# Graph attention passes: the segment's open-node factor is spread over partitions at the end of a round instead of the start of the next

## The chip, the cores and the metric

The kernel runs on one core of a Trainium2 chip, as one launch. The metric is the device time of that launch in microseconds (us). "Time before" is the median of three runs. The engines are named as the profile names them: PE is TensorE's matmul stream, PEld its weight loads, DVE is VectorE, ACT is ScalarE, POOL is GpSimd and SP the sync engine's DMA queue.

## The reference

The program computes four graph layers on 3125 nodes of 256 features and 50000 edges sorted by target node (`dst`), each followed by a residual and a layer norm. Two of the four are attention layers, and only these have to do with the change. Layer 1 has 4 heads of 64, layer 2 has 8 heads of 64. Cut to the core both do this:

```python
score = f(edge)                                    # [E, heads]
m     = segment_max(score, tgt, num_segments=n)
ex    = exp(score - m[tgt])
denom = segment_sum(ex, tgt)
alpha = ex / denom[tgt]
out   = segment_sum(alpha[..., None] * msg_edge, tgt)   # [n, heads, 64]
```

In layer 1 the score is a dot product of a gathered key row with the target's query, in layer 2 a leaky sum of one number of the source and one of the target.

## The kernel before, in words

Edges stand in NCH = 416 chunks of 128, grouped so that a chunk belongs to one tile of 128 target nodes. `Attend` runs one attention layer over all chunks; `Attend1` (4 heads) and `Attend2` (8 heads) set its tables. They are called the first and the second pass here. Work goes in NW = 26 rounds of WIN = 16 chunks. POOL gathers one row per edge into a ring of 36 slots. While round w is weighed and summed, the scores of round w + 1 are made.

A segment is a run of edges with one target node. The maximum of a segment may reach over several chunks and over a round's end. In every round a chain of small DVE steps (`CHAIN`, `chain`: "run", "most", "ends_in", "open", "ahead", "both", "picked", "edge", "most_1", "most_2", "fall", "below") finds the maximum of each segment inside the 16 chunks and the maximum carried in. Four PE instructions serve it (`TURNS`: "score", "ends", "spread", "back"). "fall" is by how much the maximum of the node that is still open at the round's start has risen since the round before. Its sum so far must be multiplied by exp(-fall), and all other nodes of that tile by 1.

Before the change that factor is made so:

- DVE compares `iota` with the open node's number (`seg.opens`, one column a round) right behind "ends_in": `open_hot`, heads x 128, at line 2238.
- ACT makes `other` = 1 - open_hot on one partition (line 2311, position `OTHER_AT`, 10 or 8 of 16). At position 14 it makes exp(-fall) and the diagonal matrix `diag` of it (lines 2314, 2316), and then the exponentials of the round's scores (line 2319).
- PE, at position 0 of the following round and behind the sum of chunk 15, multiplies open_hot by diag and adds other x ones (`scale_up`, lines 2369 and 2370). That gives a factor for each node and head in PSUM (bank `SMALL`, columns 128 on).
- DVE, at position 2, multiplies the accumulated tile by it (`rescale`, lines 2517 to 2521 and 2613 to 2619), before it adds chunk 0 of the round (`add_up`, lines 2515 and 2611).

The order on each engine is written out by hand: each engine has one program, in which the 16 positions i of a round are unrolled. PE at position i does the sum of the chunk before (`total(n - 1)`, lines 2512 and 2605), at i = 1, 5, 9, 13 four transposes for the one-hot rows of a later group (line 2334), then the fetches of query or score rows for the next round (lines 2457 and 2559), then a step of the chain, then at i = 0 `scale_up`. DVE at position i adds the chunk of two positions earlier. A sum may start when the add three chunks (first pass) or two chunks (second pass) before it is done (`SUMS`). An add waits for the add before it to have ended. ACT weighs the gathered rows of each chunk by its exponentials: in the first pass all four heads (line 2508), in the second four of the eight (line 2600), the other four being DVE's (line 2589). Every four chunks it casts the turned one-hots (line 2298).

The numbers of the open nodes come from `Segments`, once, while layer 1's tables are made: the local target number of each chunk's first edge is written to memory and read back onto 8 partitions (line 2037), and `vector_ends` copies each 16th to `opens` (line 2021).

Of the kernel before, what the change touches and what calls it, by code (L numbers as in the profile page):

```python
# [1944 lines left out]
class Segments:  # L1945
# [3 lines left out]
    def __init__(self, b, ctx, slot_rows):  # L1949
        sb = lambda n, s, d=F32: b.sb(n, s, d, ctx)  # L1950
        self.links = sb("links", [H2, NCH + 1, 2], BF16)
        self.opens = sb("opens", [H2, NW])
        self.masks = b.dram("masks", [NCH, 4 * P], BF16)
        self.hots = slot_rows.hots
        self.ends = b.dram("chunk_ends", [3, NCH])
        shared = [s for half in b.arrived for s in half]
        self.arrived = shared + [b.sem(f"slot{k}") for k in range(len(shared), RING)]
        self.before = [b.past] * len(shared) + [0] * (RING - len(shared))
        self.uses = [2 * len(range(k, NCH, RING)) for k in range(len(shared))]
        b.past = [b.past + n for n in self.uses]  # L1960
        self.passes, self.sems = 0, {}
        self.b = b
        self.turned, self.kept, self.stored, self.back = (b.sem(f"segments_{n}") for n in ("turned", "kept", "stored", "back"))
# [15 lines left out]
    def open_tables(self, b, own, spare, lent):  # L1979

        self.same = spare[0:CP, 0:3 * CG * P].rearrange("c (m g q) -> c m g q", m=3, g=CG)
        at = CG * P
        self.key = lent[0:CP, 0:at].rearrange("c (g q) -> c g q", g=CG)
        self.segs = lent[0:CP, at:3 * at].bitcast(BF16).rearrange("c (g m q) -> c g m q", g=CG, m=4)
        self.first, self.last, self.local_f = (lent[0:H2, 3 * at + k * NCH:3 * at + (k + 1) * NCH] for k in range(3))
        self.local_0 = b.sb("seg_local0", [CP, CG], F32, own)
# [26 lines left out]
    def vector_ends(self, e):  # L2013

        kept, finish = self.kept, self.finish
        e.wait_ge(self.back, 16 * 3)
        e.memset(self.links[:, 0, 0:1], 0.0)
        e.memset(self.links[:, NCH, 0:2], 0.0)
        e.tensor_tensor(self.links[:, 1:NCH, 0], self.first[:, 1:NCH], self.last[:, 0:NCH - 1], ALU.is_equal)
        e.tensor_tensor(self.links[:, 0:NCH, 1], self.first[:, :], self.last[:, :], ALU.is_equal)  # L2020
        e.tensor_copy(self.opens[:, :], self.local_f[:, 0:NCH:WIN]).then_inc(kept, 1)
        e.wait_ge(kept, 4)
        finish(e, self.links[:, :, :], self.links[:, :, :]).then_inc(kept, 1)
        e.wait_ge(kept, 5)

    def sync(self, e):
# [9 lines left out]
        e.dma_start(self.last[:, :], on_all(self.ends[1], H2)).then_inc(self.back, 16)  # L2036
        e.dma_start(self.local_f[:, :], on_all(self.ends[2], H2)).then_inc(self.back, 16)
        e.wait_ge(self.back, 48)


class Attend:


    def __init__(self, b, seg, own, name, heads, acc, table, word, stride, parts, x, lent=0):
# [23 lines left out]
        self.fall, self.keep_r, self.diag = sb("fall", [H, 1]), sb("keep_r", [H, 1]), sb("diag", [H, H])  # L2068
        self.open_hot, self.other = sb("open_hot", [H, P]), sb("other", [H, P])
        self.hot_in, self.mask_in = [sem(f"hot_in{k}") for k in range(self.HOTS)], [sem("mask_in0"), sem("mask_in1")]  # L2070
# [5 lines left out]
        self.hot_made, self.weighed, self.weighed_v = sem("hot_made"), sem("weighed"), sem("weighed_v")  # L2076
        self.summed, self.added, self.rescaled = sem("summed"), sem("added"), sem("rescaled")
        self.prep = b.sem(f"{name}_constants")

    HOTS = 6  # L2080

    STEPS = ("run", "most", "ends_in", "open", "ahead", "both", "picked", "edge", "most_1", "most_2", "fall", "below")

# [103 lines left out]
    def vector(self, e):  # L2187
# [6 lines left out]
        def add(n):  # L2194

            if n % 8 == 0:
                at["slots"] = self.slots(e, regs, n)
            tile = b.tile(self.acc, at["slots"][n % 8])
            if n % WIN == 0:
                w = n // WIN  # L2200
                e.wait_ge(self.scale_out, self.w0 + w + 1)
                if n:
                    e.wait_ge(self.added, self.c0 + n)
                self.rescale(e, tile, b.ps[:, self.SMALL, 128:128 + H]).then_inc(self.rescaled, 1)
                e.wait_ge(self.rescaled, self.w0 + w + 1)
            e.wait_ge(self.summed, self.c0 + n + 1)
            if n % WIN:
                e.wait_ge(self.added, self.c0 + n)
            self.add_up(e, tile, n).then_inc(self.added, 1)

        def chain(w, i, late):
# [19 lines left out]
            if at == here["ends_in"]:  # L2231
                after("most")
                step("ends_in", e.tensor_tensor(self.ends_in[:, :, :], self.k1[:, :].unsqueeze(2).to_broadcast([R, WIN, 2]),
                                                self.most[:, 0:P:P - 1].unsqueeze(1).to_broadcast([R, WIN, 2]), ALU.mult))
                d0 = seg.opens[0:H, w:w + 1]
                if w:
                    e.wait_ge(self.scale_out, self.w0 + w)
                step("open", e.tensor_scalar(self.open_hot[:, :], b.iota[0:H, :], d0, None, ALU.is_equal))
            if at == here["ahead"]:
# [49 lines left out]
    def scalar(self, e):  # L2289
# [10 lines left out]
        for w in range(NW + 1):  # L2300
            for i in range(WIN):
# [5 lines left out]
                if n % GRP_H == self.HOT_AT and 0 <= n // GRP_H + 1 < NCH // GRP_H:  # L2307
                    hot_rows(n // GRP_H + 1)
                if w < NW and i == self.OTHER_AT:
                    e.wait_ge(self.chain, self.chained(w, "open"))  # L2310
                    e.activation(self.other[0:1, :], self.open_hot[0:1, :], ACT.Identity, scale=-1.0, bias=self.b.ones[0:1, 0:1])
                if w < NW and i == WIN - 2:
# [9 lines left out]
    def tensor(self, e):  # L2322
# [40 lines left out]
        def scale_up(w):  # L2363
# [4 lines left out]
            e.wait_ge(self.kept_r, 2 * (self.w0 + w + 1))  # L2368
            e.matmul(small[:, 128:128 + H], self.open_hot[:, :], self.diag[:, :], start=True, stop=False)
            e.matmul(small[:, 128:128 + H], self.other[0:1, :], b.ones[0:1, 0:H], start=False, stop=True).then_inc(self.scale_out, 1)  # L2370

# [9 lines left out]
        for w in range(NW + 1):  # L2381
            for i in range(WIN):
# [8 lines left out]
                if w < NW:  # L2391
                    chain(w, i)
                if n >= 0 and i == 0:
                    scale_up(w - 1)
        total(NCH - 1)
# [15 lines left out]
class Attend1(Attend):  # L2411
# [15 lines left out]
    FETCHES = {5: [(1, 0)], 7: [(1, 1)], 10: [(1, 2)], 13: [(1, 3)], 14: [(1, 4)], 15: [(1, 5)], 1: [(0, 6)], 2: [(0, 7)]}  # L2427
    TURNS, HOT_AT, OTHER_AT = {"score": 5, "ends": 7, "spread": 10, "back": 12}, 3, 10
    CHAIN = {"run": (5, True), "most": (6, False), "ends_in": (6, True), "ahead": (8, False), "both": (8, True), "picked": (10, True), "most_1": (11, False), "fall": (11, True), "below": (12, False)}
# [94 lines left out]
class Attend2(Attend):  # L2524
# [5 lines left out]
    FETCHES = {8 + k: [(1, k)] for k in range(WIN // 2)}  # L2530
    TURNS, HOT_AT, OTHER_AT = {"score": 3, "ends": 7, "spread": 10, "back": 13}, 2, 8
    CHAIN = {"run": (4, True), "most": (5, True), "ends_in": (6, True), "ahead": (8, False), "both": (8, True), "picked": (11, True), "most_1": (12, True), "fall": (13, False), "below": (14, False)}
# [1282 lines left out]
```

## Time and profile before

| what | value |
|---|---|
| median of three runs | 3374.53 us (3372.24 to 3376.14) |
| the profiled execution | 3374.38 us, its span 3372.5 us |
| PE busy | 2869.2 us (85%) |
| DVE busy | 2490.2 us (74%) |
| ACT busy | 1936.3 us (57%) |
| POOL busy | 2164.4 us (64%) |
| DMA | 651.43 MB, mean 193 GB/s |

The span is the time between the first and the last recorded work of the profiled execution; the rest of its time lies around it. Busy shares are means over stages that have different limits. The two attention passes are two of the stages, so their rows are read by windows of time, and within a round by the timeline.

### The profile page before, as it was taken

How to read it: one execution, taken by the hardware profiler on the slowest of the kernel's cores; microseconds unless marked ns; L12 is line 12 of the kernel's file. 1: busy time of each engine (PE TensorE's matmuls, PEld its weight loads, DVE VectorE, ACT ScalarE, POOL GpSimd, SP SyncE). 2: the span in 40 equal slices, each digit the busy share in tenths (PEclk: the TensorE clock that was granted, in tenths of full speed). 3: DMA queues.
4: the chain of work that ended last, by engine and by line, in shares of the span. 5: the costliest groups of instructions: out<-in, count | busy, mean ns of one | idle time of the engine just before them, and what ended most of it. 6: DMA issues, size and time to landing. Idle time of an engine off the chain costs nothing. (4 is left out here: it accounts for less than half of the span.)

```text
span 3372.5 us, 60092 instructions
## 1 busy us (share of the span) xinstructions
PE 2869.2 (85%) x15715; PEld 1820.4 (54%) x15715; DVE 2490.2 (74%) x6119; ACT 1936.3 (57%) x6284; POOL 2164.4 (64%) x2289
## 2 busy tenths in 40 slices
PE   5799899999989797788888695999999897988776
PEld 4666555555556454455555453777777653333332
DVE  8799889999977554799998743888888774444444
ACT  0478745555542354589998621888888653333333
POOL 1777677777766541777777365777777215777774
PEclk9999989999999899799999897999999995555665
DMA  5334488888860688888777545777777354333334
GB/s 175 105 100 127 122 263 264 265 263 263 264 171 30 197 321 360 258 260 246 240 238 229 145 169 183 235 231 230 231 232 231 82 233 145 103 103 103 103 103 104
DMA packets 260603, 651.43 MB, mean 193 GB/s; under 512 B 66782, under 2 KB 115627, under 8 KB 253499
## 3 DMA queue, kind: packets, MB, share of 16 engines
q0 software_dynamic: 141840, 474.50, 46.5%
q1 hardware_dynamic: 118442, 173.08, 15.7%
q8 instruction: 150, 2.46, 0.3%
q14 instruction: 171, 1.39, 0.1%
HBM read 505.42 MB, written 145.27 MB: 193 GB/s over the span
## 5 line engine op out<-in xcount | busy, mean ns | idle before, releaser
L2127 POOL DMA_INDIRECT a_rows<-table,met x568 | 548.9, 966 | 213.7 <-issue 135.3
L3705 PE MATMUL ps<-rows_in,hot_w 128*128 128x256 f32 x832 | 450.3, 655 | 96.0 <-ACT hot_w L3667 53.3
L1330 POOL DMA_INDIRECT rows_in<-table,met x416 | 411.8, 990 | 142.7 <-issue 90.3
L3655 POOL DMA_INDIRECT rows_in<-table,met x416 | 405.0, 974 | 143.6 <-issue 120.9
L3730 DVE TENSOR_TENSOR xs<-xs,ps 128x256 f32 x416 | 175.3, 422 | 303.9 <-PE ps L3705 299.8
L3705 PEld LDWEIGHTS ps<-rows_in,hot_w 128*128 128x128 f32 x832 | 200.1, 295 | 346.2 <-ACT hot_w L3667 185.7
L3667 ACT ACTIVATE hot_w<-hot,met 128x128 f32<-128x128 f32 x416 | 166.6, 401 | 373.0 <-PE ps L3705 353.0
L2605 PE MATMUL ps<-a_rows,a_hot 128*128 128x260 f32 x1136 | 316.6, 403 | 18.1 <-DVE acc L2611 12.6
L2611 DVE TENSOR_TENSOR acc<-acc,ps 128x520 f32 x416 | 287.3, 691 | 51.5 <-PE ps L2605 44.1
L833 POOL DMA_INDIRECT records<-rec,rows x241 | 257.5, 1068 | 88.8 <-issue 72.6
L2127 POOL DMA_INDIRECT xs<-table,met x264 | 255.1, 966 | 90.0 <-issue 61.5
L2600 ACT ACTIVATE a_rows<-a_rows 128x64 f32<-128x64 f32 x1136 | 281.2, 335 | 0.0
L2508 ACT ACTIVATE a_rows<-a_rows 128x64 f32<-128x64 f32 x1104 | 274.2, 335 | 0.0
L1362 ACT ACTIVATE z<-z 128x512 f32<-128x512 f32 x208 | 131.1, 630 | 237.2 <-DVE z L1491 237.2
L1440 PE MATMUL ps<-rows_in,hot_w 128*128 128x272 f32 x832 | 244.8, 417 | 3.6 <-ACT hot_w L1377 3.6
L1403 PE MATMUL ps<-by_dst,hot_t 128*128 x1248 | 212.8, 279 | 34.2 <-issue 31.6
L2605 PEld LDWEIGHTS ps<-a_rows,a_hot 128*128 128x128 f32 x1136 | 194.4, 191 | 67.6 <-issue 32.7
L1476 DVE TENSOR_TENSOR acc<-acc,ps 128x272 f32 x416 | 181.0, 435 | 47.5 <-DVE acc L1476 41.2
L2457 PE MATMUL ps<-q_parts,a_hot_t 128*128 x1248 | 189.0, 290 | 18.8 <-DVE a_prod L2471 10.0
L2515 DVE TENSOR_TENSOR acc<-acc,ps 128x260 f32 x416 | 173.2, 416 | 40.6 <-PE ps L2512 24.8
L620 ACT ACTIVATE film_room<-film_room,code_parts 128x128 bf16<-128x128 bf16 x648 | 191.8, 388 | 19.7 <-DVE film_room L716 18.0
L2512 PE MATMUL ps<-a_rows,a_hot 128*128 128x260 f32 x568 | 183.8, 418 | 18.1 <-DVE acc L2515 9.8
(483 smaller groups left out, 6309.1 us busy)
## 6 DMA issues: line engine op xcount, KB each, us to landing
a_hot_t<-one_hots SPq DMA_DIRECT2D x104, 256.0 KB, 5.4
table<-stage SPq DMA_DIRECT2D x25, 1024.0 KB, 3.8
rows_in<-table,met POOLq DMA_INDIRECT x832, 3.7
one_hots<-hot_t SPq DMA_DIRECT2D x52, 256.0 KB
dst_row<-slot_rows SPq DMA_DIRECT2D x51, 256.0 KB, 5.0
by_dst<-dst_rows SPq DMA_DIRECT2D x25, 512.0 KB, 5.7
by_dst<-lo_rows SPq DMA_DIRECT2D x24, 512.0 KB, 4.6
a_rows<-table,met POOLq DMA_INDIRECT x568, 3.9
```

The source lines that it names most:

```text
L620: last = e.mul(r.scaled[:, m % r.RING, j, :], r.lane_hot[:, blk % 2, i, :], r.parts[:, blk, i, j // 3, j % 3:j % 3 + 1])
L833: e.indirect_dma_start(b.meta, bass.IndirectOffsetOnAxis(ap=r.rows[:, c:c + 1], axis=0), r.rec[:, c, :], None).then_inc(s, 16)
L1330: e.indirect_dma_start(self.rows[:, n % self.RING, 0:2 * D], None, self.table, bass.IndirectOffsetOnAxis(ap=self.b.met[:, n, R_SRC:R_SRC + ...
L1403: e.matmul(out, self.hot_t[:, half, k, :], row[:, m * D:(m + 1) * D], start=(m == 0), stop=False)
L1440: e.matmul(b.ps[:, 4 + n % 4, 0:D + ET], self.hot_w[:, n % self.AHEAD, :], self.rows[:, n % self.RING, D:2 * D + ET], start=True, stop=Tru ...
L2127: e.indirect_dma_start(self.row(n, 0, self.width), None, self.table, bass.IndirectOffsetOnAxis(ap=b.met[:, n, self.word:self.word + 1], ax ...
L2508: last = e.mul(value, value, row[:, 2 * D + h:2 * D + h + 1])
L2600: last = e.mul(value, value, row[:, h:h + 1])
L2605: last = e.matmul(self.b.ps[:, 2 + 2 * (n % 2) + g, 0:GW2], hot, self.group(n, g), start=True, stop=True)
L2611: return e.tensor_tensor(both, both, self.b.ps[:, at:at + G2, 0:GW2], ALU.add)
L3655: e.indirect_dma_start(self.rows[:, n % self.RING, :], None, self.table, bass.IndirectOffsetOnAxis(ap=self.b.met[:, n, R_REL:R_REL + 1], a ...
L3705: e.matmul(b.ps[:, n % self.BANKS, 0:D], self.hot_w[:, n % GRP_H, :], self.rows[:, n % self.RING, :], start=True, stop=True).then_inc(self ...
```

## The change

The number of the open node is compared once for all 26 rounds, on 128 partitions: `opened[:, 0, w]` is 1 on the partition of the node that is open at the start of round w, `opened[:, 1, w]` is 1 minus that. The chain has no step "open", and ACT makes no `other`. `scale_up` is one matmul of ones by `diag`, which puts exp(-fall) of every head on all partitions. It is issued at position 15 of the round in which exp(-fall) was made, behind the fetches of that position. At position 0 of the next round, behind the weighing of that chunk, ACT reads it from PSUM and makes `factor` = value x opened + (1 - opened) in SBUF. DVE's `rescale` waits for that and reads the factor from SBUF.

```diff
-        self.opens = sb("opens", [H2, NW])
+        self.opened = sb("opened", [P, 2, NW])
...
-        e.tensor_copy(self.opens[:, :], self.local_f[:, 0:NCH:WIN]).then_inc(kept, 1)
+        e.tensor_scalar(self.opened[:, 0, :], self.local_f[:, 0:NCH:WIN], b.part_f[:, :], None, ALU.is_equal).then_inc(kept, 1)
         e.wait_ge(kept, 4)
+        e.tensor_scalar(self.opened[:, 1, :], self.opened[:, 0, :], -1.0, 1.0, ALU.mult, ALU.add)
...
-        e.dma_start(self.local_f[:, :], on_all(self.ends[2], H2)).then_inc(self.back, 16)
+        e.dma_start(self.local_f[:, :], on_all(self.ends[2], P)).then_inc(self.back, 16)
...
-        self.open_hot, self.other = sb("open_hot", [H, P]), sb("other", [H, P])
+        self.factor = sb("factor", [P, H])
+        self.factored = b.counted("act_5", NW)
...
             if n % WIN == 0:
                 w = n // WIN
-                e.wait_ge(self.scale_out, self.w0 + w + 1)
+                e.wait_ge(*self.factored.at(w + 1))
...
-                self.rescale(e, tile, b.ps[:, self.SMALL, 128:128 + H]).then_inc(self.rescaled, 1)
+                self.rescale(e, tile, self.factor[:, :]).then_inc(self.rescaled, 1)
...
-                d0 = seg.opens[0:H, w:w + 1]
-                if w:
-                    e.wait_ge(self.scale_out, self.w0 + w)
-                step("open", e.tensor_scalar(self.open_hot[:, :], b.iota[0:H, :], d0, None, ALU.is_equal))
...
-                if w < NW and i == self.OTHER_AT:
-                    e.wait_ge(self.chain, self.chained(w, "open"))
-                    e.activation(self.other[0:1, :], self.open_hot[0:1, :], ACT.Identity, scale=-1.0, bias=self.b.ones[0:1, 0:1])
+                if n >= 0 and i == self.FACTOR_AT:
+                    now = self.seg.opened[:, :, w - 1:w]
+                    e.wait_ge(self.scale_out, self.w0 + w)
+                    if w > 1:
+                        e.wait_ge(self.rescaled, self.w0 + w - 1)
+                    e.activation(self.factor[:, :], self.b.ps[:, self.SMALL, 128:128 + H], ACT.Identity, scale=now[:, 0, :],
+                                 bias=now[:, 1, :]).then_inc(self.factored.sem, 1)
...
-            e.matmul(small[:, 128:128 + H], self.open_hot[:, :], self.diag[:, :], start=True, stop=False)
-            e.matmul(small[:, 128:128 + H], self.other[0:1, :], b.ones[0:1, 0:H], start=False, stop=True).then_inc(self.scale_out, 1)
+            e.matmul(small[:, 128:128 + H], b.ones[0:H, :], self.diag[:, :], start=True, stop=True).then_inc(self.scale_out, 1)
...
-                if n >= 0 and i == 0:
-                    scale_up(w - 1)
+                if w < NW and i == WIN - 1:
+                    scale_up(w)
```

`FACTOR_AT` is 0 in both passes.

## Rows read from the trace of the kernel before

**Rows 1.** Windows: busy us (instructions) of PE, PEld, DVE, ACT, POOL; clock, DMA, GB/s.

```profile
1384.48:1916.66 532.18, 449.13 (x2678) 303.24 (x2676) 475.15 (x1072) 471.96 (x1853) 370.23 (x390) 0.97 0.76 229
2111.63:2671.00 559.37, 530.06 (x3482) 395.57 (x3482) 490.53 (x1044) 481.61 (x1884) 384.63 (x396) 1.00 0.76 219
...
1816.00:1888.00 72.00, 63.78 (x363) 44.28 (x364) 63.50 (x142) 61.11 (x244) 48.07 (x51) 0.88 0.78 212
```

**Rows 2.** Timeline of PE at a round's end, second pass: start, us, engine, line, operation.

```profile
2392.40 0.30 PE L2559 MATMUL ps<-a_parts,a_hot_t 128*128 x6
2392.55 1.12 PE L2605 MATMUL ps<-xs,a_hot 128*128 128x260 f32 x4
2393.61 0.38 PE L2369 MATMUL ps<-a_diag,a_open_hot 8*128 8x8 f32 x2
...
2394.14 1.14 PE L2605 MATMUL ps<-xs,a_hot 128*128 128x260 f32 x4
...
2396.66 0.68 PE L2605 MATMUL ps<-xs,a_hot 128*128 128x260 f32 x2 [0.22 <-DVE acc L2611]
```

**Rows 3.** Timeline of DVE in the same round.

```profile
2393.82 0.70 DVE L2611 TENSOR_TENSOR acc<-acc,ps 128x520 f32 x1 [0.41 <-PE ps L2605]
...
2400.88 0.69 DVE L2611 TENSOR_TENSOR acc<-acc,ps 128x520 f32 x1
...
2401.78 0.69 DVE L2611 TENSOR_TENSOR acc<-acc,ps 128x520 f32 x1
```

**Rows 4.** Timeline of PE: fetch and sum with and without the spread between them.

```profile
2385.57 0.29 PE L2559 MATMUL ps<-a_parts,a_hot_t 128*128 x6
2385.79 0.40 PE L2358 MATMUL ps<-a_both,a_to_rows 8*128 8x32 f32 x2
2386.13 1.14 PE L2605 MATMUL ps<-a_rows,a_hot 128*128 128x260 f32 x4
2387.11 0.29 PE L2559 MATMUL ps<-a_parts,a_hot_t 128*128 x6
2387.26 1.12 PE L2605 MATMUL ps<-a_rows,a_hot 128*128 128x260 f32 x4
```

**Rows 5.** Timeline of ACT in the second pass, position 2.

```profile
2395.60 0.59 ACT L2298 CAST a_hot<-ps 128x512 f32<-128x512 bf16 x1 [0.40 <-PE ps L2334]
```

**Rows 6.** Timeline of all engines at a round's end, first pass.

```profile
1574.10 3.92 ACT L2508 ACTIVATE a_rows<-a_rows 128x64 f32<-128x64 f32 x16
...
1576.15 0.60 PE L2512 MATMUL ps<-xs,a_hot 128*128 128x260 f32 x2
...
1577.58 0.43 DVE L2515 TENSOR_TENSOR acc<-acc,ps 128x260 f32 x1 [0.21 <-DVE acc L2515]
```

**Rows 7.** Timeline of DVE in the first pass, position 6.

```profile
1585.17 0.39 DVE L2515 TENSOR_TENSOR acc<-acc,ps 128x260 f32 x1
...
1585.61 0.27 DVE L2238 TENSOR_SCALAR a_open_hot<-iota,opens 4x128 f32<-4x128 f32 x1
1585.80 0.40 DVE L2515 TENSOR_TENSOR acc<-acc,ps 128x260 f32 x1
```

**Rows 8.** Waits of ACT in the first pass: us in total, times, longest.

```profile
ACT a_keep_r L2314 <- DVE a_fall L2260: 35.1, 24, 1.8
```

**Rows 9.** Timeline of DVE in the first pass, a round at a lowered clock.

```profile
1824.02 0.43 DVE L2515 TENSOR_TENSOR acc<-acc,ps 128x260 f32 x1 [0.81 <-PE ps L2512]
```

**Rows 10.** Groups of the whole run by line, shapes apart: busy us, mean ns, idle.

```profile
L1370 ACT ACTIVATE weight<-bend,ones,edge_scale 128x4 f32<-128x4 f32 x104 | 40.4, 388 | 3.4
...
L2311 ACT ACTIVATE a_other<-a_open_hot,ones 1x128 f32<-1x128 f32 x52 | 20.1, 386 | 83.0 <-DVE a_open_hot L2238 83.0
```

**Rows 11.** Groups of DVE in the second pass.

```profile
L2589 DVE TENSOR_TENSOR a_rows<-a_rows 128x512 f32<-128x512 f32 x132 | 89.8, 681 | 0.0
...
L2619 DVE TENSOR_TENSOR acc<-acc,ps 128x512 f32 x25 | 17.0, 682 | 0.0
```

**Rows 12.** Single lines of the table stage: duration min/median/max, first and last start.

```profile
L2021 DVE COPY opens<-xs x1: 366/366/366, 1225.0 to 1225.0; 8x26 f32<-8x26 f32 x1
```

More of the change, by code:

```diff
@@ L1984, in open_tables @@
         self.segs = lent[0:CP, at:3 * at].bitcast(BF16).rearrange("c (g m q) -> c g m q", g=CG, m=4)
-        self.first, self.last, self.local_f = (lent[0:H2, 3 * at + k * NCH:3 * at + (k + 1) * NCH] for k in range(3))
+        self.first, self.last, self.local_f = (lent[0:n, 3 * at + k * NCH:3 * at + (k + 1) * NCH] for k, n in enumerate((H2, H2, P)))
         self.local_0 = b.sb("seg_local0", [CP, CG], F32, own)
@@ L2013, in vector_ends @@
     def vector_ends(self, e):
-        kept, finish = self.kept, self.finish
+        b, kept, finish = self.b, self.kept, self.finish
         e.wait_ge(self.back, 16 * 3)
@@ L2077, in __init__ @@
         self.summed, self.added, self.rescaled = sem("summed"), sem("added"), sem("rescaled")
+        self.factored = b.counted("act_5", NW)
         self.prep = b.sem(f"{name}_constants")
     HOTS = 6
-    STEPS = ("run", "most", "ends_in", "open", "ahead", "both", "picked", "edge", "most_1", "most_2", "fall", "below")
+    STEPS = ("run", "most", "ends_in", "ahead", "both", "picked", "edge", "most_1", "most_2", "fall", "below")
     def in_order(self, table, ahead):
@@ L2427 @@
     FETCHES = {5: [(1, 0)], 7: [(1, 1)], 10: [(1, 2)], 13: [(1, 3)], 14: [(1, 4)], 15: [(1, 5)], 1: [(0, 6)], 2: [(0, 7)]}
-    TURNS, HOT_AT, OTHER_AT = {"score": 5, "ends": 7, "spread": 10, "back": 12}, 3, 10
+    TURNS, HOT_AT, FACTOR_AT = {"score": 5, "ends": 7, "spread": 10, "back": 12}, 3, 0
     CHAIN = {"run": (5, True), "most": (6, False), "ends_in": (6, True), "ahead": (8, False), "both": (8, True), "picked": (10, True), "most_1": (11, False), "fall": (11, True), "below": (12, False)}
@@ L2530 @@
     FETCHES = {8 + k: [(1, k)] for k in range(WIN // 2)}
-    TURNS, HOT_AT, OTHER_AT = {"score": 3, "ends": 7, "spread": 10, "back": 13}, 2, 8
+    TURNS, HOT_AT, FACTOR_AT = {"score": 3, "ends": 7, "spread": 10, "back": 13}, 2, 0
     CHAIN = {"run": (4, True), "most": (5, True), "ends_in": (6, True), "ahead": (8, False), "both": (8, True), "picked": (11, True), "most_1": (12, True), "fall": (13, False), "below": (14, False)}
```

## The prediction

> **What bounds the kernel now.** I read the windows first, to cut out the two stages that the change touches, then each engine's waits in them, then the timeline of a steady round. The rows that a sentence rests on are named by group.
>
> The two passes take 532 and 559 us of the span, some 20.5 and 21.4 us a round [rows 1]. Nothing outside them changes but a few instructions of setup. In the second pass PE is busy for 530 of 559 us, DVE for 491, ACT for 482. That looks like a PE-bound stage, but a busy share doesn't say where in the round PE is the one waited for, and this change moves PE work from one place in the round to another. So the timeline decides.
>
> Second pass, end of a round: PE issues the fetches of position 15 at 2392.40, the sum of chunk 15 at 2392.55, then the two pairs of `scale_up` at 2393.61, the sum of chunk 0 at 2394.14. Two sums later, at 2396.66, it waits 0.22 us for a DVE add [rows 2]. DVE stood idle for 0.41 us until the sum of chunk 15 was there, at 2393.82 [rows 3]. From there DVE never idles up to the add at 2400.88, whose end releases a PE sum again; the rescale is in that stretch. So the loop of a round is: PE up to the sum of chunk 15, DVE from the add of chunk 15 for some 7.8 us, PE again. `scale_up` now lies behind the sum of chunk 15, in the stretch where PE has time: removing it there gains nothing, since PE waits for DVE soon after. The wait of about 0.4 us at this add stands in 23 of the 25 rounds between 2130 and 2660; in the other two it is 0.21.
>
> First pass: DVE is the bound nearly all round. At the same point the add of chunk 15 waits 0.21 us on DVE's own add before it and not on PE [rows 6], and so in some 20 rounds. In three of the last rounds, where the clock granted to PE is 0.88 on average instead of 1.00, that add waits for PE's sum: 0.81 us in the worst [rows 1, 9], 0.67 and 0.37 in the others.
>
> **The change part by part.**
>
> 1. `scale_up` moves ahead of the sum of chunk 15, and is one matmul (two instructions) instead of two. Its price there is how much later the sum starts. The nearest row is the spread, which also has 8 rows and 128 columns of weights, and also stands between a fetch and a sum: fetch to sum is 2386.13 - 2385.57 = 0.56 us with the spread between, and 2387.26 - 2387.11 = 0.15 us without: 0.41 us [rows 4]. The new matmul moves 8 columns instead of 32, so it is at most that. From the other side, the two pairs of before took 2394.14 - 2393.61 = 0.53 us, half of it 0.27 [rows 2]. I take 0.38, close to the row with the same neighbours. All of it is on the path, since DVE already waits for that sum. Second pass: 24 rounds x 0.38 = +9.1 us. First pass: 3 rounds x 0.38 = +1.1 us; in the other rounds it is covered: PE's sum of chunk 15 started at 1576.15 and took 0.60, DVE takes it at 1577.58 [rows 6], 0.8 us later. If that cover were gone in all 20 rounds, it would be 7.6 us more.
>
>    The Trainium skill, TensorE: Matmul & The Clock Gate, section Step-by-step: what each phase is for, says that PE may pull a weight load ahead of matmuls in flight. By it the new weight load would hide under the fetches and the price would be nearer to 0.27, the sum nearer to 3381. The row of the spread shows its first matmul 0.22 us behind the fetches' start and the sum 0.34 behind that, so little is hidden there.
>
> 2. The second matmul pair goes: 0.27 us a round of PE work, in a place where PE waits for DVE afterwards (0.22 us at 2396.66 already) [rows 2]. Value 0 in both passes; if it were on the path, -0.27 x 26 = -7 us a pass.
>
> 3. DVE's `open_hot` goes. It lasts 0.27 us, and the add behind it starts 0.19 us after it [rows 7]. But that add has to wait for the end of the add before, and adds that follow each other directly show 0.21 us from end to start [rows 6]: 1585.17 + 0.39 + 0.21 = 1585.77, against 1585.80 [rows 7]. So 0.03 us goes, not 0.19. In the second pass 2400.88 + 0.69 + 0.21 = 2401.78 is the start itself [rows 3]: nothing. Sum: 20 x 0.03 = -0.6 us. Upper bound of the gain 0.19 x 50 = 9.5 us.
>
> 4. ACT: `other` (0.386 us) goes, `factor` comes: 128 x heads with a scale and a bias from memory, as the row of 128 x 4 with both, 0.388 us [rows 10]. Equal in busy time, but it moves to position 0 and adds a wait for PE. Queued behind it are the weighings of chunks 1 to 15. Second pass: ACT was through with chunk 2 at 2395.60 - 0.40 [rows 5], so with chunk 0 two times 0.98 us earlier, at 2393.2; PE's matmul, issued behind the fetches of 2392.40, would end near 2393.0 [rows 2], so no stall; the 0.39 us fit into the 0.40 us that the cast at position 2 waits for PE [rows 5]. First pass: ACT is through with chunk 0 at 1574.10 + 3.92/4 = 1575.08, PE's matmul comes at 1576.15 and ends 0.4 later [rows 6]: a stall of some 1.5 us, plus 0.3. ACT has waited 35.1/24 = 1.46 us a round for "fall" [rows 8], and `other` gives 0.39 back before it, so the round's exponentials come as before. In between, chunk by chunk, the weighing still ends 0.6 us or more ahead of PE's sum. Value 0; if the slack fails, 0.4 x 20 = +8 us. In the last round of each pass ACT is waited for: +0.3 us together.
>
> 5. Rescale waits for `factor` instead of `scale_out`. In the second pass it is ready near 2393.7, and DVE gets to it after 2395: 0. It reads the factor from SBUF: DVE on SBUF alone takes 681 ns for 128 x 512, and the rescale with a PSUM operand 682 [rows 11]: 0.
>
>    The Trainium skill, VectorE: DVE Perf Modes, section on the TRN2 errata, gives an instruction that reads PSUM 62 cycles more than one from SBUF, an estimate of 65 ns for each of two rescale instructions in 52 rounds, or -6.7 us. The two rows differ by 1 ns, so the trace doesn't agree and nothing of this is in the sum.
>
> 6. Setup: one copy of 0.37 us becomes two instructions on 128 x 26, and the load is broadcast to 128 partitions instead of 8. They stand at 1225 us, in the stage that makes layer 1's tables [rows 12], where DVE has room between PE's results and does not wait for this load. 0; one more instruction of that size, 0.4 us, is the most.
>
> Sum: 9.1 + 1.1 - 0.6 + 0.3 = +9.9 us. The profiled execution took 3374.38 us (span 3372.5 and 1.9 around it), 0.15 us under the median of 3374.53. The forecast is **3384 us**, 0.3% slower. By the two ends of the price of `scale_up`, 0.27 and 0.41 over 27 rounds, it is 3381 to 3386.
>
> **Rivals.**
>
> - *PE is the bound of the second pass, wherever its work stands.* For it: 530 of 559 us busy, granted clock 1.00 [rows 1]. Then a pair less is what counts: 26 x 0.27 = 7 us less, **3367 us**. It decides if DVE's 0.41 us wait at the add of chunk 15 doesn't grow. Against it: that wait, and PE's own at 2396.66 [rows 2, 3]. This is the one that ends faster.
> - *The DVE step is worth its full distance.* 0.19 us x 50 = -9.5 us [rows 7], which cancels the loss: **3375 us**. It needs the adds not to wait on each other, against the 0.21 us that such pairs show [rows 6].
> - *ACT's stall comes through in the first pass.* The 1.5 us stall is as large as the mean slack of 1.46 [rows 6, 8], and rounds differ. At 0.4 us for 20 rounds: **3392 us**.
> - *PE's clock in the first pass.* In its last rounds the granted clock sank to 0.88 on average [rows 1], after PE had stood idle for "most_2". A thinner PE stream around the round's end could bring other rounds there; each would cost up to the 0.81 us wait [rows 9], for half of 20 rounds +8 us: **3392 us**. Or the late rounds could be spared, for -2.
>
> **How the numbers follow.** Forecast 0.55; PE-bound and faster 0.12; DVE step at full worth 0.14; ACT's stall 0.10; clock 0.09. The range 3370 to 3393 holds the forecast, the cancelled case and most of the two last; it leaves out the faster case and their tails. The likeliest case's own range is 3380 to 3388. A change of 0.2%, 6.7 us, is about what a measurement of this kernel can tell from none. Slower by more than that: forecast and the two last, less the low ends of each, 0.68. Within it: the cancelled case and those low ends, 0.19. Faster: 0.13.
>
> **What would show it.** Right: in the second pass the add of chunk 15 (line 2611 at a round's end) waits some 0.8 us for PE instead of 0.41, the first sum behind the fetches of position 15 starts 0.53 us after them instead of 0.15, and the window from the first weighing to the last add is about 9 us longer than 559; the first pass is within 2 us of 532. ACT waits some 1.5 us for PE before `factor` in the first pass and almost not for "fall" any more. Right on the DVE step: adds at position 7 start 0.21 us behind the end of the add before. Wrong: the second pass as long as before or shorter, or a first pass that moves by more than the second.

## The result and the profile after

The changed kernel takes 3389.71 us, median of 5 runs (3382.10 to 3391.20), the one before 3372.72, median of 5 (3368.57 to 3376.14). The ratio is 1.0036, 95% interval [1.0023, 1.0049]: slower, by 0.23% to 0.49%. The forecast was 3384, slower. In two of the experiments below one run took 2.5% and 30% longer than the others of its kernel; the ratios leave these two out, the medians don't. The profiled execution took 3391.20 us with a span of 3389.4, against 3374.38 and 3372.5.

The windows of the changed kernel, cut by the same events as [rows 1]: first weighing to last add of the first pass, then of the second, then what lies between the passes, then all that follows (columns as in [rows 1]). The third number from the end is the granted clock, the share of TensorE's full speed: 1.00 is the upper of its two levels (2.4 GHz), 0.50 the lower (1.2 GHz), and a number between them is a mean over the stretch.

```profile
1384.70:1922.76 538.06, 450.08 (x2626) 301.90 (x2624) 472.40 (x1047) 466.50 (x1854) 369.83 (x390) 0.96 0.75 227
2115.86:2686.39 570.53, 523.26 (x3430) 394.21 (x3430) 488.40 (x1019) 478.49 (x1885) 390.43 (x396) 0.99 0.74 215
...
1922.76:2115.86 193.10, 123.99 (x559) 79.67 (x560) 75.20 (x290) 43.48 (x95) 111.65 (x146) 0.81 0.57 186
2686.39:3389.40 703.01, 579.17 (x1607) 276.57 (x1607) 340.03 (x787) 245.10 (x592) 425.84 (x466) 0.61 0.40 120
```

The second pass is 11.2 us longer (570.53 against 559.37), though PE is busy in it for 523.3 us instead of 530.1. The first pass is 5.9 us longer (538.06 against 532.18). The last two windows were 194.97 and 701.50 before: -1.9 and +1.5. With 0.2 at the start that is the whole difference of the spans, 16.9 us.

The round end of [rows 2 and 3], in the changed kernel: PE, then DVE.

```profile
2400.58 0.30 PE L2560 MATMUL ps<-a_parts,a_hot_t 128*128 x6
2400.81 0.38 PE L2371 MATMUL ps<-a_diag,ones 8*128 8x8 f32 x2
2401.12 2.02 PE L2606 MATMUL ps<-xs,a_hot 128*128 128x260 f32 x8
...
2405.26 1.11 PE L2606 MATMUL ps<-xs,a_hot 128*128 128x260 f32 x4 [0.89 <-DVE acc L2612]
```

```profile
2402.41 0.70 DVE L2612 TENSOR_TENSOR acc<-acc,ps 128x520 f32 x1 [0.81 <-PE ps L2606]
2403.02 0.68 DVE L2590 TENSOR_TENSOR xs<-xs 128x512 f32<-128x512 f32 x1
2403.62 0.16 DVE L2618 TENSOR_TENSOR acc<-acc,a_factor 128x8 f32 x1
2403.70 0.68 DVE L2620 TENSOR_TENSOR acc<-acc,a_factor 128x512 f32 x1
```

From the fetch of position 15 to the sum of chunk 15 it is 2401.12 - 2400.58 = 0.54 us, before 0.15: the matmul in between costs 0.39. The add of chunk 15 waits 0.81 us for PE, before 0.41. What PE saved behind that sum it loses at once: it waits 0.89 us for DVE a few sums later, before 0.22. The weight loads (PEld) of the sum of chunk 15 show what changed at that spot, first in the changed kernel, then in the experiment "scale behind the sum" below, where nothing lies between fetch and sum:

```profile
2401.12 0.52 PEld L2606 LDWEIGHTS ps<-xs,a_hot 128*128 128x128 f32 x3
```

```profile
2399.30 0.74 PEld L2606 LDWEIGHTS ps<-xs,a_hot 128*128 128x128 f32 x4
```

Straight behind the fetches of 2399.18 to 2399.47 the load starts at 2399.30, while the last fetch is still running. Behind the small matmul of 2400.81 to 2401.19 it starts only at 2401.12, near that matmul's end.

The first pass at full clock, the round end of [rows 6] and the position of [rows 7]: ACT with the new step, then DVE.

```profile
1577.84 1.06 ACT L2509 ACTIVATE a_rows<-a_rows 128x64 f32<-128x64 f32 x4
1580.42 0.35 ACT L2312 ACTIVATE a_factor<-ps,opened 128x4 f32<-128x4 f32 x1 [1.52 <-PE ps L2371]
```

```profile
1588.92 0.39 DVE L2516 TENSOR_TENSOR acc<-acc,ps 128x260 f32 x1
1589.24 0.20 DVE L2235 TENSOR_TENSOR a_ends_in<-a_k,a_most 64x32 f32<-64x32 f32 x1
1589.53 0.43 DVE L2516 TENSOR_TENSOR acc<-acc,ps 128x260 f32 x1
```

ACT waits 1.52 us for the factor's matmul. DVE's comparison of 0.27 us is gone, yet from add to add it is 0.61 us, before 0.63. ACT's waits in the whole first pass (total, times, longest), for [rows 8]:

```profile
ACT a_factor L2312 <- PE ps L2371: 47.6, 25, 3.8
ACT a_keep_r L2316 <- DVE a_fall L2258: 15.8, 24, 1.5
```

The wait for "fall" went from 35.1 to 15.8 us: ACT's new stall took the place of half of it.

Last, a first-pass round in which TensorE's clock was for some time at the lower of its levels: a window of it, then PE, ACT, DVE.

```profile
1428.00:1434.00 6.00, 5.90 (x23) 4.11 (x24) 4.89 (x11) 3.26 (x14) 3.88 (x5) 0.50 0.82 269
```

```profile
1428.04 0.36 PE L2363 MATMUL ps<-ident,a_most 64*128 64x64 f32 x1 [1.91 <-DVE a_most L2254]
...
1429.89 1.49 PE L2458 MATMUL ps<-q_parts,a_hot_t 128*128 x6
...
1432.03 1.48 PE L2458 MATMUL ps<-q_parts,a_hot_t 128*128 x6
...
1436.63 0.82 PE L2458 MATMUL ps<-q_parts,a_hot_t 128*128 x6
```

```profile
1435.54 0.35 ACT L2312 ACTIVATE a_factor<-ps,opened 128x4 f32<-128x4 f32 x1 [3.81 <-PE ps L2371]
```

```profile
1431.51 0.69 DVE L2472 TENSOR_TENSOR a_prod<-ps,a_rows 128x512 f32<-128x512 f32 x1 [0.79 <-PE ps L2458]
...
1436.28 0.42 DVE L2516 TENSOR_TENSOR acc<-acc,ps 128x260 f32 x1 [1.32 <-PE ps L2513]
```

PE stands idle for 1.91 us until "most_2" is there, and after that six fetches take 1.49 us instead of 0.82 as at 1436.63, with the clock up again. DVE, the bound of this pass, then waits for PE twice, 2.1 us in sum, and the round lasts 22.64 us (from the rescale at 1415.90 to the one at 1438.54) instead of 20.5.

How long a round is can be read from one rescale of DVE to the next. 24 full rounds of each pass, worked out from those starts, for every kernel run on a chip where the median of the kernel before is 3373 to 3375 us. A round is called long if it lies over 0.6 us above the median, and low if the granted clock over it is under 1.00. The medians are taken with the 25th round, the last one, in. "Rest" is the mean of the rounds that are not low, those at full clock from end to end:

```
kernel             first pass: sum  long  low   rest     second pass: sum   median   rest
before                       495.4     4    5  20.47                518.6    21.41  21.49
changed                      499.6     7    7  20.44                527.5    21.87  21.89
scale behind sum             500.6     6   10  20.46                516.9    21.48  21.49
only moved                   497.3     5    5  20.51                532.8    21.98  22.05
DVE step kept                500.3     7    6  20.47                525.5    21.77  21.79
factor later                 496.4     5    5  20.44                528.4    21.78  21.84
before, filled               492.8     2    1  20.45                518.0    21.31  21.46
matmul twice                 492.6     1    1  20.49                536.4    21.98  22.05
```

The columns "rest" are the comparison without the clock: the changed kernel is 0.40 us a round longer in the second pass and not longer at all in the first.

### The profile page after: what moved, and what is told of

Read it like the earlier page. It is cut to its first block and busy times, and to the rows that moved or that the text cites. A ratio compares the mean times of both kernels' runs of the same rounds, so it can differ in the third digit from the quotient of the medians.

```text
span 3389.4 us, 59883 instructions
## 1 busy us (share of the span) xinstructions
PE 2875.4 (85%) x15611; PEld 1821.2 (54%) x15611; DVE 2486.4 (73%) x6068; ACT 1926.2 (57%) x6284; POOL 2170.9 (64%) x2289
## 5 line engine op out<-in xcount | busy, mean ns | idle before, releaser
L3706 PE MATMUL ps<-rows_in,hot_w 128*128 128x256 f32 x832 | 465.6, 672 | 82.1 <-ACT hot_w L3668 35.7
L2606 PE MATMUL ps<-a_rows,a_hot 128*128 128x260 f32 x1136 | 313.7, 402 | 29.3 <-DVE acc L2612 22.5
L2296 ACT CAST a_hot<-ps 128x512 f32<-128x512 bf16 x208 | 119.4, 574 | 139.3 <-PE ps L2336 138.8
```

Of the source, the lines that this page charges most:

```text
L2606: last = e.matmul(self.b.ps[:, 2 + 2 * (n % 2) + g, 0:GW2], hot, self.group(n, g), start=True, stop=True)
L3706: e.matmul(b.ps[:, n % self.BANKS, 0:D], self.hot_w[:, n % GRP_H, :], self.rows[:, n % self.RING, :], start=True, stop=True).then_inc(self ...
```

## The experiments

Six of the runs were on two slow chips, where the kernel before itself takes 3914.58 and 3859.99 us; their times are compared only with those.

**Scale behind the sum.** The changed kernel with `scale_up` back in its old place; nothing else of the change is undone. The factor moves two chunks on in the first pass and one in the second, since its matmul now comes later.

```
-                if w < NW and i == WIN - 1:
-                    scale_up(w)
+                if n >= 0 and i == 0:
+                    scale_up(w - 1)
...
-    TURNS, HOT_AT, FACTOR_AT = {...}, 3, 0
+    TURNS, HOT_AT, FACTOR_AT = {...}, 3, 2
...
-    TURNS, HOT_AT, FACTOR_AT = {...}, 2, 0
+    TURNS, HOT_AT, FACTOR_AT = {...}, 2, 1
```

> The changed kernel with the one matmul of the factor put back behind the sum of chunk 15 (position 0 of the next round); ACT makes the factor two positions later in the first pass and one later in the second, so that it need not wait for PE. Everything else of the change stays. Theory of the place (the matmul costs because it stands ahead of the sum that DVE waits for): the 25 rounds of the second pass, from first to last rescale, take 540 us as before the change (551 after it), the add of chunk 15 waits 0.41 us again instead of 0.81, and the time is that of before, 3373 +- 3. Rival, ACT's factor step or its wait is what costs: it is still there, so the second pass stays near 551 and the time near 3385. Rival, the clock of PE in the first pass: the second pass comes back, the first keeps its 5 to 6 us in some executions.

Measured: 3378.34 us, median of 11, beside 3375.18 of the kernel before (18 runs); ratio 1.0007 [0.9997, 1.0017]. That is 2 us over the 3370 to 3376 that I expected: the second pass came back and the first stayed long in this profile, as the last rival says. Its second pass, first add to last, and below it the same window of the kernel before, of the changed one and of the next experiment, a fence for each kernel:

```profile
2122.22:2678.65 556.43, 521.26 (x3423) 387.80 (x3421) 485.65 (x1014) 476.63 (x1872) 386.88 (x393) 1.00 0.75 219
```

```profile
2114.95:2670.59 555.64, 527.02 (x3474) 393.19 (x3471) 488.48 (x1039) 478.64 (x1872) 381.93 (x393) 1.00 0.75 219
```

```profile
2119.19:2685.98 566.79, 520.63 (x3423) 392.25 (x3421) 486.19 (x1014) 475.27 (x1872) 387.61 (x393) 1.00 0.74 215
```

```profile
2120.20:2690.04 569.84, 525.85 (x3474) 397.87 (x3471) 488.18 (x1039) 478.62 (x1872) 376.69 (x393) 1.00 0.74 214
```

The second pass is back: 556.4 us, before 555.6, changed 566.8. Its 24 rounds sum to 516.9, 10.6 less than in the changed kernel. On DVE the wait is 0.41 again and on PE fetch and sum are 0.15 apart:

```profile
2400.60 0.69 DVE L2612 TENSOR_TENSOR acc<-acc,ps 128x520 f32 x1 [0.41 <-PE ps L2606]
```

```profile
2399.18 0.29 PE L2560 MATMUL ps<-a_parts,a_hot_t 128*128 x6
2399.33 1.12 PE L2606 MATMUL ps<-xs,a_hot 128*128 128x260 f32 x4
2400.38 0.38 PE L2371 MATMUL ps<-a_diag,ones 8*128 8x8 f32 x2
```

So the loss of the second pass is the place of that matmul. (ACT's factor step moved too here; the next experiment has no such step.) With the place undone, all the rest (a matmul pair less, a DVE step less, the one-hots made once) gains nothing either: PE's 5.8 us less of work, 521.3 against 527.0, lie beside other waits.

**Only moved.** The kernel before with the move alone; both matmuls of `scale_up` stay.

```
-                if n >= 0 and i == 0:
-                    scale_up(w - 1)
+                if w < NW and i == WIN - 1:
+                    scale_up(w)
```

> The kernel before with one edit: both matmuls of the factor are issued at position 15 of the round, ahead of the sum of chunk 15. The one-hots, ACT's other and the rescale from PSUM are as before. Theory of the place: two matmuls ahead of that sum cost 0.41 + 0.25 = about 0.66 us a round of the second pass, so its 25 rounds take 540 + 24 x 0.66 = 556 us, the add of chunk 15 waits about 1.07 us, and the time is 3373 + 16 for the second pass + 1 to 6 for the first = 3390 to 3395. Rival, ACT's factor step costs: it isn't in this kernel, so 3373 and 540 us.

Measured: 3390.91 us, ratio 1.0048 [1.0034, 1.0063]. Second pass, 24 rounds: 532.8, that is +14.2 over the kernel before, 0.59 a round (0.56 in the rounds at full clock). One round's PE and DVE:

```profile
2405.33 0.30 PE L2559 MATMUL ps<-a_parts,a_hot_t 128*128 x6
2405.56 0.38 PE L2369 MATMUL ps<-a_diag,a_open_hot 8*128 8x8 f32 x2
2405.80 0.36 PE L2370 MATMUL ps<-ones,a_other 1*128 1x8 f32 x2
2406.09 2.02 PE L2605 MATMUL ps<-xs,a_hot 128*128 128x260 f32 x8
```

```profile
2407.38 0.69 DVE L2611 TENSOR_TENSOR acc<-acc,ps 128x520 f32 x1 [1.03 <-PE ps L2605]
```

Fetch to sum is 0.76 us and the wait 1.03, a little under the 0.66 us a round and the 1.07 expected. The move makes the loss without any other part of the change, and it grows with the number of matmuls that are moved, read from the wait of DVE: none 0.41, one 0.81, two 1.03.

**DVE step kept.** The changed kernel with the comparison still issued in the chain of steps, its result read by nobody.

```
-    STEPS = ("run", "most", "ends_in", "ahead", ...)
+    STEPS = ("run", "most", "ends_in", "open", "ahead", ...)
...
+                if w:
+                    e.wait_ge(self.scale_out, self.w0 + w)
+                step("open", e.tensor_scalar(self.open_hot[:, :], b.iota[0:H, :], b.part_f[0:H, :], None, ALU.is_equal))
```

> The changed kernel with a DVE compare of heads x 128 put back at the place of the step that was removed, with its wait and semaphore; nothing reads its result. Theory, the step was covered by the wait of one add for the end of the add before: no change against the changed kernel (3388 +- 3), steady rounds of the first pass 20.3 us as in both kernels (at most 0.03 longer). Rival, the step is worth the 0.19 us between its start and the next: 0.19 x 51 = 9.7 us more, 3398, and rounds of 20.5 in the first pass.

Measured: 3388.79 us, ratio 1.0044 [1.0031, 1.0058], as the changed kernel. DVE at the same position:

```profile
1585.58 0.39 DVE L2520 TENSOR_TENSOR acc<-acc,ps 128x260 f32 x1
1585.89 0.20 DVE L2236 TENSOR_TENSOR a_ends_in<-a_k,a_most 64x32 f32<-64x32 f32 x1
1586.02 0.27 DVE L2240 TENSOR_SCALAR a_open_hot<-iota,part_f 4x128 f32<-4x128 f32 x1
1586.21 0.40 DVE L2520 TENSOR_TENSOR acc<-acc,ps 128x260 f32 x1
```

Add to add 0.63 us, and 0.61 without the step. The rounds are not longer, in the first pass (20.47 us at full clock against 20.44) or in the second (21.79 against 21.89). A step that lies in the 0.21 us between two dependent adds is free here, and so its removal is worth nothing.

**Factor later.** The changed kernel with ACT's factor behind two more chunks in the first pass, where it need not wait.

```
-    TURNS, HOT_AT, FACTOR_AT = {...}, 3, 0
+    TURNS, HOT_AT, FACTOR_AT = {...}, 3, 2
```

> The changed kernel with ACT's factor step of the first pass at position 2 instead of 0, behind two more weighings: PE's matmul is long done there, so ACT's 1.5 us wait a round (45.5 us in all) goes. Theory, that wait is covered by the wait for the maximum's fall later in the round: steady rounds of the first pass stay 20.3 us, the time stays within 2 us of the changed kernel, and ACT waits 35 us for the fall again instead of 16. Rival, ACT's stall comes through in the first pass and makes its 5 to 6 us: the first pass loses them and the time falls to 3383.

Measured: 3384.87 us, median of 7, ratio 1.0031 [1.0020, 1.0043]. ACT's waits in the first pass:

```profile
ACT a_keep_r L2316 <- DVE a_fall L2258: 36.0, 24, 1.7
ACT a_hot L2296 <- PE ps L2336: 19.2, 41, 4.4
ACT a_factor L2312 <- PE ps L2371: 4.2, 6, 1.8
```

The stall at the factor is gone (47.6 to 4.2 us) and the waits of before are back, 36.0 for "fall". The median round is 20.53 in both, and the mean at full clock 20.44. The time was expected within 2 us of the changed kernel's; it is 4.8 us lower in the medians and 1.7 by the ratios, with intervals that overlap; 3.2 us stand in the first pass of the profile, which had 5 long rounds instead of 7. The mean granted clock of the 7 runs is 0.892, in the 5 of the changed kernel 0.889. So the difference goes the same way as the clock. Whether the stall brings lowered rounds on, or these executions had fewer by chance, is not shown.

**Fillers.** To test the clock: four matmuls of 128x128 into an unused part of PSUM, read by nobody, ahead of the transpose for which PE waits on "most_2", in the first pass only. They go into the kernel before, into the changed one, and into "scale behind the sum"; beside them the changed kernel with the factor's matmul issued twice, which is the price of one more matmul in the place.

```
             if i == self.TURNS["back"]:
+                if self.name == "a1" and w >= 2:
+                    for _ in range(4):
+                        e.matmul(b.ps[:, self.BACK, 3 * P:4 * P], b.ident[:, :], b.ones[:, :], start=True, stop=True)
...
+            e.matmul(small[:, 128:128 + H], b.ones[0:H, :], self.diag[:, :], start=True, stop=True)
             e.matmul(small[:, 128:128 + H], b.ones[0:H, :], self.diag[:, :], start=True, stop=True).then_inc(self.scale_out, 1)
```

> The kernel before with four extra matmuls of 128x128 a round in the first pass (from its third round on), issued ahead of the transpose that waits for most_2, where PE stands idle for 1.9 us; their result is read by nobody. Theory of the clock: PE is granted half its clock now and then in the first pass because of that idle gap, and then DVE waits for it. With the gap filled no stretch of the first pass after 1415 us shows a granted clock under 1.00, the 24 steady rounds take 490 to 492 us instead of 495, and the time falls by 3 to 5 us. Rival, the gap has nothing to do with the clock: dips and the time stay, or the fillers cost 0.2 us and more a round, 5 us.

> The changed kernel with the same four fillers. If its first pass is 5 us longer only by dips of the clock (six to seven rounds of over 21 us against four), it falls to the same 490 to 492 us for 24 rounds, 8 us less, and the whole is 3389 - 8 = 3381, the loss of the second pass (9 us) left. Rival, the matmul ahead of the sum or ACT's stall costs in the first pass too at full clock: the 24 rounds stay 3 us or more above those of the kernel before with fillers.

> The changed kernel with the matmul of the factor behind the sum of chunk 15, ACT's factor step later, and the fillers: both causes taken away. By both theories 540 us for the 25 rounds of the second pass, 490 to 492 for the 24 of the first: 3378 - 8 = 3370, below the kernel before. Rival, the moved step does something else: it stays at 3378.

> The changed kernel with the matmul of the factor issued twice in its new place. Theory of the place: each further one costs what it adds to PE's stream, 0.25 us (the distance of the two pairs in the kernel before was 0.21 to 0.24), so the 24 steady rounds of the second pass take 527 + 6 = 533 us, the same as the kernel in which both old matmuls were only moved, and the add of chunk 15 waits 1.05 us instead of 0.81. Rival, DVE's time is what makes these rounds 0.4 longer: no change.

Measured, on a chip where the kernel before takes 3914.58 us: before filled 3946.10, ratio 1.0081 [1.0049, 1.0112]; changed filled 3966.17, 1.0122 [1.0090, 1.0154]; behind the sum and filled 3940.53, 1.0067 [1.0041, 1.0094]; matmul twice 3953.87, 1.0101 [1.0069, 1.0134]. There the fillers cost: the kernel before is 0.8% slower with them. (24 rounds of the first pass last 629 to 643 us in the three kernels with fillers and 611 in "matmul twice", which has none.) That answers nothing of the clock on an ordinary chip, so all four were run again: two on an ordinary chip, and two, as it turned out, on another slow one.

**Before filled, again.**

> The kernel before with four extra matmuls of 128x128 a round in the first pass, ahead of the transpose that waits for most_2 (read by nobody), once more: in its first run every kernel of that call took 16% longer, the kernel before too (3915 us), with slower gathers and PE's clock at 0.84 in the first pass. Theory of the clock, where the kernel before takes 3373 to 3378: no dip of the granted clock in the first pass after 1415 us, 24 steady rounds in 490 to 492 us instead of 495, 3 to 5 us less. Rival: the fillers only add PE work to a stretch in which PE is soon wanted: 0.2 us and more a round, 5 us and more longer.

Measured, beside a kernel before of 3375.17 us (17 runs): 3369.32, median of 12, ratio 0.9979 [0.9970, 0.9987]: faster, 4 to 10 us, and the only kernel here that is. A stretch inside the first pass, 1415 to 1895 us, of it, of the kernel before and of the changed one (the clock is third from the end), then PE at "back":

```profile
1415.00:1895.00 480.00, 422.04 (x2677) 298.18 (x2675) 438.31 (x982) 434.41 (x1707) 353.06 (x370) 1.00 0.80 241
```

```profile
1415.00:1895.00 480.00, 404.05 (x2457) 274.21 (x2454) 435.78 (x979) 431.38 (x1697) 347.33 (x365) 0.98 0.79 237
```

```profile
1415.00:1895.00 480.00, 402.70 (x2402) 272.18 (x2399) 429.59 (x947) 421.95 (x1680) 346.88 (x365) 0.97 0.79 237
```

```profile
1595.68 1.05 PE L2362 MATMUL ps<-ones,ident 128*128 128x128 f32 x8
1597.74 0.27 PE L2364 MATMUL ps<-ident,a_most 64*128 64x64 f32 x1 [1.01 <-DVE a_most L2256]
```

PE's idle time there is 1.01 us instead of about 1.9, the granted clock 1.00 instead of 0.98, the long rounds 2 instead of 4, and the first pass 2.6 us shorter over its 24 rounds (492.8 us, just over the 490 to 492 expected). At full clock the rounds are the same, 20.45 and 20.47. The gain in the median is firm; that it comes by the clock rests on one profile of each kernel, which show 2.6 of the 5.9 us, and on the mean granted clock over whole runs, 0.8925 with fillers (12 runs) and 0.8895 without (17).

**Matmul twice, again.**

> The changed kernel with the matmul of the factor issued twice in its new place, once more. Theory of the place, where the kernel before takes 3373 to 3378: 24 rounds of the second pass 533 us (527 changed, 518.6 before), as in the kernel where both old matmuls were moved (532.8), the add of chunk 15 waits 1.05 us, the time is 6 us above the changed kernel, 3391 to 3395. Rival, the length of these rounds is DVE's: no change against the changed kernel.

Measured: 3389.57 us, ratio 1.0039 [1.0026, 1.0052]. The time is that of the changed kernel, 3389.71, and not 6 us more; the profile has the loss in the second pass and gets it back in the first. Its second pass has a median round of 21.98 us, as "only moved" (which also has two matmuls there), against 21.87: a second matmul costs 0.1 in the median, 0.16 in the rounds at full clock, and 0.22 in the wait of DVE, 1.03. The add of a steady round, and the wait for a gather that lies in its one round of 29.26 us and so in the sum of 536.4:

```profile
2120.79 0.23 DVE L2571 TENSOR_TENSOR a_total<-ps,a_rows 128x64 f32<-128x64 f32 x1 [3.73 <-DMA xs<-table,met]
...
2407.45 0.69 DVE L2613 TENSOR_TENSOR acc<-acc,ps 128x520 f32 x1 [1.03 <-PE ps L2607]
```

The first pass came out otherwise than in any profile of the changed kernel: 24 rounds in 492.6 us with one long round, at a granted clock of 1.00, in a kernel that has the moved matmuls and ACT's stall and no fillers:

```profile
1415.00:1895.00 480.00, 401.15 (x2489) 274.87 (x2487) 434.99 (x957) 426.04 (x1699) 348.95 (x369) 1.00 0.80 240
```

So at full clock the change costs the first pass nothing, as the column "rest" of the table says for every kernel. How much the clock sinks differs from execution to execution of one and the same kernel: of the 18 runs of the kernel before that stand beside "scale behind the sum", the seven of under 3373 us had a mean granted clock over the whole run of 0.892 to 0.897, the seven of over 3377 us one of 0.883 to 0.890.

**Changed filled and behind filled, again.**

> The changed kernel with the four fillers of the first pass, once more (the kernel before with them took 3369 us, 0.21% less than without). If the changed kernel's first pass is longer only by dips of PE's clock, its 24 steady rounds come to within 1 us of those of the kernel before with fillers, and the whole to 3369 + 9 to 12 (the second pass) = 3378 to 3381. Rival, the moved matmul or ACT's stall costs in the first pass at full clock: 3 us and more above.

> The changed kernel with the matmul of the factor behind the sum of chunk 15, ACT's factor step later, and the fillers, once more: both causes taken away. Second pass 540 us for 25 rounds, first pass as in the kernel before with fillers, 3368 to 3371, 5 us below the kernel before. Rival, without the fillers this kernel took 0.07% more than the kernel before, and that part is not the clock: 3372 and more.

Measured, on a chip where the kernel before takes 3859.99 us: 3926.10, ratio 1.0154 [1.0120, 1.0187], and 3894.74, ratio 1.0092 [1.0063, 1.0121]. Of the clock on ordinary chips this again tells nothing: the version that should be best there, `scale_up` behind the sum with fillers, is not measured on one. The place of `scale_up` counts for more on such a chip: first rescale to last of the second pass is 660.1 us with it ahead of the sum and 627.5 behind, 32.6 us over 25 rounds, 1.3 us a round; on the chip of 3914.58 us it is 659.4 and 633.5. The rounds at full clock are only 0.35 us apart (25.05 and 24.70; 25.40 and 25.02 on the other chip), which is the price of the one matmul again. The rest goes with the clock: 18 of 24 rounds are low with the matmul ahead of the sum and 7 with it behind (16 and 11 on the other chip). Why there are more of them is not shown.

## Why the prediction was right, point by point

The forecast of 3384, slower, had the right sign and the right place; the time came out 6 us higher and the rise 7 us larger (17.0 by the medians instead of 9.9). Step by step, by the numbers of the prediction:

1. *Place of `scale_up`.* Second pass: forecast 0.38 x 24 = +9.1, measured 527.5 - 518.6 = +8.9 over 24 rounds (0.40 a round at full clock), and the whole window +11.2, of which 1.9 is the last round. "Scale behind the sum" and "only moved" show the cause by undoing it and by doing it alone. The price, taken from the spread, was 0.38 and came out at 0.39 (0.54 - 0.15). By the Trainium skill, TensorE: Matmul & The Clock Gate, section Step-by-step: what each phase is for, the weight load may be pulled ahead of matmuls in flight. The trace agrees where the sum follows the fetches (2399.30, while the last fetch runs) and not where it follows the small matmul (2401.12), and the price is 0.39 and not 0.27. In the late rounds of the first pass the matmul has its price too: in a round with the clock down that add waits 1.22 and 1.32 us in the changed kernel and 0.81 in the one before. How many such rounds there are is the clock's part, see below.
2. *A matmul pair less.* Forecast 0. Its work is missing from PE's busy time (5.8 us of the second pass in "scale behind the sum"), and the time of that pass stays within 0.8 us. Right.
3. *DVE's comparison.* Forecast -0.6 us in sum. The step kept changes no round: 0.63 against 0.61 us from add to add. Right, and the rival of -9.5 us is out: with the step put back the time is 3388.79 us and not 9.7 more.
4. *ACT.* The stall was forecast at 1.5 us and is 1.52, and it takes its room from the wait for "fall", which was forecast to be almost gone and kept 15.8 of 35.1 us. At full clock it is covered: the median round is 20.53 with the stall and without it. The rival that the stall comes through for 0.4 us a round is out. Last rounds: forecast +0.3, but the last of the first pass took 17.42 instead of 15.98, the last of the second 23.4 instead of 21.46. The first goes with the clock, at 0.80 over it instead of 0.89: "DVE step kept", with the whole change in it, has 15.84 at 0.89. The second has a wait for a gather (1.39 us), a lowered clock and one DVE instruction of 1.22 us instead of 0.68 in it, and "matmul twice" has 21.89 there; so neither is shown to be the change's.
5. *Rescale from SBUF.* Forecast 0. The rescales of 128x512 with the factor from SBUF, shortest, median and longest in ns:

```profile
L2620 DVE TENSOR_TENSOR acc<-acc,a_factor x26: 681/683/1221, 2117.4 to 2668.3; 128x512 f32 x26
```

   The median is 683 ns; before it was 682 with a PSUM operand, as is the mean in [rows 11]. By the table in the Trainium skill, VectorE: DVE Perf Modes, section on the TRN2 errata, an estimate says that it should have become some 65 ns shorter; the trace doesn't agree. Right.
6. *Setup.* The start of the first pass moved by 0.2 us. Right.

What was mis-sized is the first pass: forecast +0.5 us (1.1 - 0.6) and a share of the 0.3 for last rounds, measured +5.9. It is not in the ordinary round, whose median is 20.51 before and 20.53 after, and whose mean at full clock is 20.47 and 20.44. It is in 7 low rounds instead of 5, which have 0.85 to 0.92 as their clock, and in the last round, which is low too. That is the rival "PE's clock in the first pass", which I had at 8 us with a chance of 0.09, and it came true in part. What I had not seen is that this term belongs to the execution and not only to the kernel: 18 runs of the kernel before differ by up to 18 us, and by and large the faster ones have the higher clock. "Matmul twice", which has all of the change's costs in the first pass and one matmul more, had one low round, "DVE step kept" 6 and "scale behind the sum" 10. Whether the change makes such rounds likelier, by the 1.5 us stall or by PE's thinner stream, stays open. The mean granted clock of whole runs gives no sign of it: 0.8892 in the 5 runs of the changed kernel, 0.8902 and 0.8895 in 18 and 17 of the one before. The window "within 2 us of 532", by which I wanted to judge my own step, was for the same reason too narrow.

Between the medians of the two kernels lie 17.0 us, and by the ratio 7.8 to 16.5. The 8.9 us of the place are the part that the experiments show. That the whole came within 6 us of the forecast owes something to luck, since the clock's part of a few runs could have been several us more or less.

## What to carry to other kernels

Work may be removed from the busiest engine and the kernel still get slower, if what is left moves ahead of the instruction that another engine is waiting for: look for the one spot in a round where the bound engine waits, and price every instruction put ahead of it in full, and what lies behind it at nothing as long as its engine waits soon after. A step that fits into the gap between two dependent instructions of one engine (0.21 us between two adds here) costs nothing, and taking it out gives nothing back. Where an engine's clock dips now and then, compare rounds at full clock with rounds at full clock before you put a sum down to the change.

## What was not expected of the hardware

- Matmuls that nobody reads made the kernel faster: 24 times four of them, in the gap before "back", went with a granted clock of 1.00 instead of 0.98 and 5.9 us off the median (3369.32 against 3375.17).
- The same kernel took 3375, 3860 and 3915 us on different chips. On the two slower ones the granted clock in the first pass was lower too, 0.90 to 0.91 from first rescale to last in the six kernels profiled there. Here is the first pass, first add to last, of "behind filled, again", with fillers at 0.91, which had 0.99 to 1.00 on the ordinary chip in the kernel before filled:

```profile
1613.38:2263.05 649.67, 503.27 (x2788) 342.10 (x2787) 473.04 (x1039) 467.34 (x1835) 360.04 (x380) 0.91 0.63 182
```

- There the fillers cost time instead of giving it (ratio 1.0081 instead of 0.9979).
